# Sandwich kernel, last units: scaled f in PSUM banks, scaling of unit 14 on ScalarE, the small steps of the last two halves interleaved

## What is computed

```python
x = x + _layernorm(attn(_layernorm(x)))      # causal convolution, gelu, projection, layer norm with gamma and beta
x = x + _layernorm(ffn(_layernorm(x)))       # the stage that this change touches, at its end
# ffn(x):
xr = mu_r * x + (1.0 - mu_r) * x_prev
xk = mu_k * x + (1.0 - mu_k) * x_prev
r = sigmoid(xr @ W_r.T)
k_act = square(relu(xk @ W_k.T))
out = r * (k_act @ W_v.T)
```

## Time and profile before

| | |
|---|---|
| Time, median of 3 runs | 155.37 us (154.94 to 155.74) |
| Time of the profiled execution | 156.3 us |
| Its span, first to last instruction | 153.7 us |
| PE busy | 139.1 us (91%) |
| DVE busy | 131.8 us (86%) |
| ACT busy | 130.1 us (85%) |
| POOL busy | 131.2 us (85%) |
| Mean granted TensorE clock, share of full speed | 0.976 |

### The profile page before, as it was taken

One profiled execution on the slowest core, in us unless ns is written; L12 is line 12 of the kernel. 1 busy time (PEld: TensorE's weight loads), 2 busy tenths in 40 slices (PEclk: granted clock), 3 DMA queues, 4 the chain that ended last, 5 costly groups with the idle time before them and its releaser, 6 DMA issues.

```text
span 153.7 us, 3286 instructions
## 1 busy us (share of the span) xinstructions
PE 139.1 (91%) x957; PEld 119.2 (78%) x957; DVE 131.8 (86%) x373; ACT 130.1 (85%) x387; POOL 131.2 (85%) x194
## 2 busy tenths in 40 slices
PE   3879998999999999999999999999999999999600
PEld 3769897989697888879977899789797788777500
DVE  1979999999999999999999699997999996333773
ACT  5749789899969899979899999779989988999800
POOL 4598959999989899999899979978889989999880
PEclk9978999999999999999999999999999999999995
DMA  3889900000000002000200002200200000422743
GB/s 91 209 227 313 339 22 2 0 0 6 0 0 0 0 4 73 0 0 0 71 1 0 0 4 70 69 4 4 68 0 0 0 0 4 139 68 68 236 134 108
DMA packets 18704, 8.98 MB, mean 58 GB/s; under 512 B 1536, under 2 KB 18688, under 8 KB 18688
## 3 DMA queue, kind: packets, MB, share of 16 engines
q1 hardware_dynamic: 18400, 8.79, 19.6%
q10 hardware_dynamic: 288, 0.00, 0.1%
HBM read 4.59 MB, written 4.19 MB: 57 GB/s over the span
## 4 chain that ended last, share of the span: by engine, by line
PE 69%; POOL 9%; ACT 6%; DVE 4%; DMA 3%; SPq 3%; issue 3%; DVEq 0%; POOLq 0%; ACTq 0%
PE ps_r L734 9%; PE ps_r L733 9%; PE ps_k L722 8%; PE ps_k L723 8%; PE ps_tv L742 8%; PE ps_z L700 7%; PE ps_prefix L683 6%; PE ps_tv L713 5%; PE ps_z L701 3%; DMA x_all<-in_x 3%; ACT xn L323 3%; PE ps_prefix L685 3%; PE ps_xT L676 3%; POOL x_r L201 2%; POOL xn_pow L214 2%
## 5 line engine op out<-in xcount | busy, mean ns | idle before, releaser
L323 ACT ACTIVATE xn<-x_all,x_bias,x_r 128x128 f32<-128x128 f32 x64 | 26.3, 489 | 2.4 <-POOL x_bias L203 2.4
L734 PE MATMUL ps_r<-mixed_T,tsT 128*128 128x128 f32 x128 | 24.7, 275 | 0.0
L733 PE MATMUL ps_r<-mixed_T,tsT 128*128 128x128 f32 x128 | 24.7, 275 | 0.0
L380 ACT ACTIVATE f_normal<-f,out_bias,yf_r 128x128 f32<-128x128 f32 x56 | 22.9, 492 | 0.5 <-POOL out_bias L256 0.5
L214 POOL TENSOR_TENSOR xn_pow<-xn,pow_token 128x512 f32<-128x512 f32 x16 | 20.4, 1278 | 3.1 <-ACT xn L323 2.1
L700 PE MATMUL ps_z<-pv_T,gelu 128*128 128x128 f32 x128 | 22.3, 276 | 0.3 <-DVE pv_T L566 0.2
L733 PEld LDWEIGHTS ps_r<-mixed_T,tsT 128*128 128x128 f32 x128 | 19.6, 192 | 1.4 <-issue 1.4
L683 PE MATMUL ps_prefix<-prefix_ones,xn_pow 128*128 128x256 f32 x64 | 19.7, 391 | 0.8 <-POOL xn_pow L214 0.8
L343 ACT ACTIVATE junk<-ps_z 128x128 f32<-128x128 f32 x64 | 16.7, 276 | 3.9 <-PE ps_z L701 3.8
L700 PEld LDWEIGHTS ps_z<-pv_T,gelu 128*128 128x128 f32 x128 | 19.3, 191 | 0.7 <-DVE pv_T L566 0.4
L495 DVE SCALAR_TENSOR_TENSOR x_all<-ps_z,yf_r,x_all 128x128 f32<-128x128 f32 x64 | 17.6, 341 | 2.6 <-POOL yf_r L235 2.5
(11 more groups left out here) (92 smaller groups left out, 367.1 us busy)
## 6 DMA issues: line engine op xcount, KB each, us to landing
out_x<-x_all SPq DMA_DIRECT2D x15, 256.0 KB, 2.3
x_all<-in_x SPq DMA_DIRECT2D x7, 512.0 KB, 6.0
x_all<-in_x SPq DMA_DIRECT2D x2, 128.0 KB, 3.0
x_all<-in_x SPq DMA_DIRECT2D x1, 256.0 KB, 3.5
out_x<-x_all SPq DMA_DIRECT2D x2, 128.0 KB, 1.8
w_pv<-in_W_proj SPq DMA_DIRECT2D x1, 64.0 KB, 2.7
w_pv<-in_W_v SPq DMA_DIRECT2D x1, 64.0 KB, 4.0
w_rk<-in_W_r SPq DMA_DIRECT2D x1, 64.0 KB, 3.6
```

The lines of the kernel that those rows point to most:

```text
L323: last = a_.activation(tile(xn[u % D], j), xa(u, j), ACT.Identity, bias=col(x_bias, u, j), scale=col(x_r, u, j))
L380: last = a_.activation(tile(f_normal[u % D], j), tile(f[u % D], j), ACT.Identity, bias=out_bias[:, u, j:j + 1], scale=yf_r[:, u, 1, j:j + 1])
L733: t_.matmul(tile(ps_r, j), tsT[u % D][:, q, l + 1:l + 1 + P], mixed_T[:, 0, :], start=True, stop=False)
L734: last = t_.matmul(tile(ps_r, j), tsT[u % D][:, q, l:l + P], mixed_T[:, 1, :], start=False, stop=True)
```

## The change

The scaled f of units 11 to 15 is no longer written to the ring `f_normal` in SBUF but to five PSUM banks that the attention part has finished with (`late_f`: `ps_xT` for unit 11, `ps_prefix` for 12, `ps_z1` for 13, `ps_z2` for 14, `ps_z0` for 15). Its writer waits for the last reader of the bank (`conv_ready` or `t_ready`) in place of the sum that freed the `f_normal` buffer. The scaling of unit 14 moves from DVE to the end of ACT's queue. The four small steps of each half on POOL become functions of their own, and `half_variance(1)` goes between the root and the means of half 0. On DVE `f_stats_half(1)` follows `gate_half(1)` directly, and the scaling and the sum of half 0 come ahead of the sum of unit 14. The diff, cut to its core:

```diff
@@ -83,6 +82,7 @@
+        late_f = [ps_xT, ps_prefix, ps_z1, ps_z2, ps_z0]
...
@@ -256,20 +255,32 @@
-            def f_scale_half(h):
+            def half_variance(h):
 
                 j = 2 * h
                 pool.wait_ge(f_half_stats, h + 1)
                 g_.tensor_scalar(f_ve[:, LAST, j:j + 2], yf_raw[:, LAST, 1, j:j + 2, 2], 1.0 / P, 4 * EPS, ALU.mult,
-                                 ALU.add).then_inc(half_chain, 1)
-                pool.wait_ge(half_chain, 3 * h + 1)
+                                 ALU.add).then_inc(half_ve, 1)
+
+            def half_root(h):
+
+                j = 2 * h
+                pool.wait_ge(half_ve, h + 1)
                 g_.tensor_tensor(yf_r[:, LAST, 1, j:j + 2], f_ve[:, LAST, j:j + 2], neg_half[:, 0:2],
-                                 ALU.pow).then_inc(half_chain, 1)
+                                 ALU.pow).then_inc(half_r, 1)
+
+            def half_means(h):
...
+            def half_bias(h):
...
@@ -300,7 +311,8 @@
-            f_scale_of(12, 2); add_f(9); add_f(10); f_scale_of(14, 1); f_scale_half(0); f_scale_half(1)
+            f_scale_of(12, 2); add_f(9); add_f(10); f_scale_of(14, 1); half_variance(0); half_root(0)
+            half_variance(1); half_means(0); half_bias(0); half_root(1); half_means(1); half_bias(1)
@@ -374,10 +386,21 @@
+            def scale_f_late(u):
+
+                act.wait_ge(f_scale, u + 1)
+                if u < SUM_ON_VECTOR + 2:
+                    act.wait_ge(conv_ready, UNITS)
+                else:
+                    act.wait_ge(t_ready, u + 1)
+                for j in range(TILES):
+                    last = a_.activation(tile(late_f[u - SUM_ON_VECTOR], j), tile(f[u % D], j), ACT.Identity,
                                          bias=out_bias[:, u, j:j + 1], scale=yf_r[:, u, 1, j:j + 1])
                 last.then_inc(f_scaled, 1)
@@ -408,8 +431,8 @@
-            copy_tT(15); square_k(14); scale_f(11); tanh_r(14); scale_f(12); relu_k(15); square_k(15); tanh_r(15)
-            scale_f(13)
+            copy_tT(15); square_k(14); scale_f_late(11); tanh_r(14); scale_f_late(12); relu_k(15); square_k(15)
+            tanh_r(15); scale_f_late(13); scale_f_late(14)
@@ -508,21 +531,9 @@
-            def scale_f_late(u):
...
             def add_f_late(u):
...
+                dve.wait_ge(f_scaled, u + 1)
+                v_.tensor_tensor(xa(u, 0, TILES), xa(u, 0, TILES), late_f[u - SUM_ON_VECTOR][:],
                                  ALU.subtract).then_inc(out_ready_late, 1)
@@ -542,17 +553,16 @@
                 dve.wait_ge(f_half_scale, h + 1)
-                after(dve, out_ready, min(LAST - D + 1, SUM_ON_VECTOR))
-                after(dve, out_ready_late, LAST - D + 1 - SUM_ON_VECTOR)
+                dve.wait_ge(t_ready, UNITS)
                 for j in range(2 * h, 2 * h + 2):
-                    last = v_.tensor_scalar(tile(f_normal[LAST % D], j), tile(f[LAST % D], j), yf_r[:, LAST, 1, j:j + 1],
+                    last = v_.tensor_scalar(tile(late_f[-1], j), tile(f[LAST % D], j), yf_r[:, LAST, 1, j:j + 1],
                                             out_bias[:, LAST, j:j + 1], ALU.mult, ALU.add)
...
-                v_.tensor_tensor(xa(LAST, 2 * h, 2), xa(LAST, 2 * h, 2), f_normal[LAST % D][:, 2 * h * P:(2 * h + 2) * P],
+                v_.tensor_tensor(xa(LAST, 2 * h, 2), xa(LAST, 2 * h, 2), late_f[-1][:, 2 * h * P:(2 * h + 2) * P],
                                  ALU.subtract).then_inc(out_half, 1)
@@ -626,9 +636,8 @@
-            f_stats_of(14); add_f_late(12); gate_half(0); f_stats_half(0); gate_half(1); scale_f_late(14)
-            f_stats_half(1); add_f_late(13); add_f_late(14); scale_f_half(0); scale_f_half(1); add_f_half(0)
-            add_f_half(1)
+            f_stats_of(14); add_f_late(12); gate_half(0); f_stats_half(0); gate_half(1); f_stats_half(1)
+            add_f_late(13); scale_f_half(0); add_f_half(0); add_f_late(14); scale_f_half(1); add_f_half(1)
```

More of the change, by code:

```diff
@@ L10 @@
 T_ON_POOL = (1, 3, 5, 7, 9, 11, 13)
-F_ON_VECTOR = 14
 SUM_ON_VECTOR = 11
@@ L110, in sandwich @@
             "f_ready", "f_stats", "f_ve_done", "f_r_done", "f_mean_done", "f_scale"))
[L111 to L115, removed]
+        f_scaled, out_ready, out_ready_late, stored = (sem(n) for n in ("f_scaled", "out_ready", "out_ready_late", "stored"))
+        f_half, f_half_stats, half_ve, half_r, half_means_done, f_half_scale, f_half_scaled, out_half = (sem(n) for n in (
+            "f_half", "f_half_stats", "half_variance", "half_root", "half_means", "f_half_scale", "f_half_scaled", "out_half"))
         block = ctx.enter_context(nc.Block())
@@ L263, in f_scale_half @@
                 g_.tensor_scalar(f_ve[:, LAST, j:j + 2], yf_raw[:, LAST, 1, j:j + 2, 2], 1.0 / P, 4 * EPS, ALU.mult,
-                                 ALU.add).then_inc(half_chain, 1)
-                pool.wait_ge(half_chain, 3 * h + 1)
+                                 ALU.add).then_inc(half_ve, 1)
+            def half_root(h):
+                j = 2 * h
+                pool.wait_ge(half_ve, h + 1)
                 g_.tensor_tensor(yf_r[:, LAST, 1, j:j + 2], f_ve[:, LAST, j:j + 2], neg_half[:, 0:2],
-                                 ALU.pow).then_inc(half_chain, 1)
+                                 ALU.pow).then_inc(half_r, 1)
+            def half_means(h):
+                j = 2 * h
                 pool.wait_ge(y_scale, UNITS)
-                pool.wait_ge(half_chain, 3 * h + 2)
+                pool.wait_ge(half_r, h + 1)
                 g_.tensor_tensor(yf_mean_r[:, LAST, :, j:j + 2], yf_raw[:, LAST, :, j:j + 2, 1],
-                                 yf_r[:, LAST, :, j:j + 2], ALU.mult).then_inc(half_chain, 1)
-                pool.wait_ge(half_chain, 3 * h + 3)
+                                 yf_r[:, LAST, :, j:j + 2], ALU.mult).then_inc(half_means_done, 1)
+            def half_bias(h):
+                j = 2 * h
+                pool.wait_ge(half_means_done, h + 1)
                 g_.tensor_tensor(out_bias[:, LAST, j:j + 2], yf_mean_r[:, LAST, 0, j:j + 2], yf_mean_r[:, LAST, 1, j:j + 2],
@@ L376, in scale_f @@
                 act.wait_ge(f_scale, u + 1)
-                after(act, out_ready, min(u - D + 1, SUM_ON_VECTOR))
-                after(act, out_ready_late, u - D + 1 - SUM_ON_VECTOR)
+                after(act, out_ready, u - D + 1)
                 for j in range(TILES):
                     last = a_.activation(tile(f_normal[u % D], j), tile(f[u % D], j), ACT.Identity,
+                                         bias=out_bias[:, u, j:j + 1], scale=yf_r[:, u, 1, j:j + 1])
+                last.then_inc(f_scaled, 1)
+            def scale_f_late(u):
[6 more added lines that the diff above has]
+                    last = a_.activation(tile(late_f[u - SUM_ON_VECTOR], j), tile(f[u % D], j), ACT.Identity,
                                          bias=out_bias[:, u, j:j + 1], scale=yf_r[:, u, 1, j:j + 1])
@@ L509, in gate @@
                                         ALU.mult).then_inc(f_ready, 1)
-            def scale_f_late(u):
[L512 to L518, removed]
-            def add_f_late(u):
[L521 to L525, removed]
+            def add_f_late(u):
+                dve.wait_ge(f_scaled, u + 1)
+                v_.tensor_tensor(xa(u, 0, TILES), xa(u, 0, TILES), late_f[u - SUM_ON_VECTOR][:],
                                  ALU.subtract).then_inc(out_ready_late, 1)
```

## The result

The changed kernel takes 153.76 us (median of 4 runs, 153.43 to 154.28) against 155.23 us before in the same comparison. The ratio is 0.990, with a 95% interval of 0.9875 to 0.9929: faster by 1.5 us, or between 1.1 and 1.9. The forecast was 154.2, 1.2 us faster.

The account below looks back on a forecast made before the run. PE was taken to bound the kernel until 143.6 us, leaving only the last 9.1 us to win in. The last store issued at 150.20 instead of 151.39 gave 155.37 - 1.19 = 154.2 us, 8-in-10 range 153.5 to 155.2.

Parts of the forecast that it names:

- The hold-up of POOL: At the kernel's end, POOL and a DVE sum with both inputs in SBUF were said to hold each other up.
- rival A: The hold-up stays, coming from both engines working on x_all or SBUF at all: gain 0.27, 155.1 us, chance 0.15.
- this stall: POOL's L273 in half 0's small steps, 1.38 us instead of 0.20: 1.18 us of the second bias's earlier time.
- the interleaving: POOL's small steps of both halves mixed: the rest of the 1.5 us by which half 1's bias comes earlier.
- the upper bound: DVE's scaling into PSUM loses the fast rate: 0.07 dearer each, 0.3 for four, 0.75 for two.
- rival C: ACT's eight scalings for units 11 and 12 are dearer into PSUM: 157.1 us at a doubled pitch, chance 0.06.
- rival B: The last stores, close together, begin later or land in 2.3 instead of 1.87: gain 0.76, 154.6 us, chance 0.14.
- the sum of 1.19: Whole gain at the kernel's end: last store issued at 150.20 against 151.39 us.

## Why the prediction came out right

| from the first half gate, us | foretold | changed kernel |
|---|---|---|
| half 0's bias ends | 2.59 | 2.57 |
| half 1's bias ends | 3.88 | 3.84 |
| half 1's scaling starts | 4.35 | 4.30 |
| last sum ends | 5.56 | 5.48 |
| span ends | 7.9 | 7.8 |

*The hold-up of POOL.* Right in kind: neither sums nor small steps are stretched once an input of the DVE sum is in PSUM, and rival A fell with the first profile after. The stretch reappears with the buffers in SBUF and with spare work that has nothing to do with x_all.

*Its share of the gain.* Left open, and easily misread. I wrote that 1.18 of the 1.5 us by which the second bias comes earlier is this stall and the rest the interleaving. For the bias that holds (5.37 before, 4.12 without the interleaving, 3.84 with it), but a reader would take the stall for the gain at the end, and there the parts do not add up like that: PSUM alone gives 0.77, all the rest without PSUM gives 1.07, both together 1.19. With PSUM alone DVE's queue is the bound, and the rest finds 0.42 to win. With the rest alone the bound is half 1's bias, a little behind DVE's queue, and PSUM finds 0.37 at the sums but pays 0.25 at the halves.

*The interleaving.* Its steps took the times foretold and it wins nothing, because DVE is later by 0.46 us than the second bias (0.2 without it; my text said 0.4, its own times give 0.47). That it depends on unit 14's scaling being off DVE I had not seen; undoing the move alone costs 0.95.

*DVE's new order.* I took it as given and priced the edit within the sum. Undone, the end is 0.2 shorter. The step that I left out was to lay out the old order beside the new one.

*Scaling into PSUM.* I took the upper bound, 0.75 for two. It is 0.73 (405 to 414 ns each), so the fast rate is indeed lost, and the rule of the Trainium skill (VectorE: DVE Perf Modes, "Why PSUM operands drop a tier") agrees. With the halves in SBUF the 0.25 comes back.

*ACT into PSUM (rival C).* Its pace is the old one, and the tanh of unit 15 starts at 143.82 with ACT idle ahead of it, so C has no part in this. No row shows ACT faster in pace for the PSUM destination either.

*The stores (rival B).* Nothing of it reached the end. Data flow without a gap behind each other, as laid out, and only half 0's store is slower to land (2.1 instead of 1.8); the last one lands after 1.8. It is issued 5.51 after the gate, 1.27 earlier than before where I had 1.19; that and the 0.1 at its landing are the 1.3 of the span.

*The whole.* The measured 1.5 us is 0.3 more than the sum of 1.19. The span after the gate became shorter by 1.3, and the remaining 0.2 is within the interval of the ratio. The terms that can be checked one by one came within 0.1, so no errors had to cancel. That two parts of the change win nothing did not hurt the forecast, since it priced the whole and no part alone; this much was luck.

## What to carry to other kernels

When two engines hold each other up, first list what each would wait for if the hold-up were gone; here the cure was worth 0.8 us alone and 0.1 net beside other edits that shortened the same stretch. Undo each part of a change that came out well: one part (the interleaving) gave nothing as long as DVE was the bound, and made the kernel depend on another, one (DVE's order) cost 0.2. A destination that frees one engine can be dearer for the engine that writes it, so choose it buffer by buffer, by what the other engine does at that moment.

## What the runs showed of the hardware

A POOL instruction that is held up by DVE is not always held for a whole row of DVE instructions. In before L273 lasted until the second of two sums had ended (148.43 against 148.37). With the buffers in SBUF, L277 got through between two sums that follow each other without a gap (it ended at 148.00, the first sum at 147.95), and the next step was held by the second (until 148.60, the sum ended at 148.54). What decides between the two cases was not tested.

A DVE tensor_scalar of 128x128 with two column operands takes 402 to 414 ns into PSUM and 335 to 347 ns into SBUF. ACT's instruction of the same shape is shorter into PSUM (445 to 463 ns in the changed kernel, against 481 to 492 for the same sixteen with the buffers in SBUF) at nearly the same pace, eight in 3.14 us against 3.17.
